# The first stage of a layered state-space and feed-forward kernel: where four small steps stand

## What is computed

```
x = x + 0.5 * (layernorm(x) @ w.T + bias)          # w: 6-bit weights, (q - zero_point) * scale
x = x + causal_convolution(layernorm(x), K0) + D0 * layernorm(x)
x = x + 0.5 * (layernorm(x) @ w.T + bias)
x = x + 0.5 * (silu(n @ W_gate.T) * (n @ W_up.T)) @ W_down.T      # n = layernorm(x)
x = x + causal_convolution(layernorm(x), K1) + D1 * layernorm(x)
x = x + 0.5 * (silu(n @ W_gate.T) * (n @ W_up.T)) @ W_down.T
```

```
denom = g[:, None] - Lambda[None, :]
cauchy = lambda v: (v[None, :] / denom).sum(-1)
k00, k01, k10, k11 = cauchy(Ct.conj() * B), cauchy(Ct.conj() * p), cauchy(q.conj() * B), cauchy(q.conj() * p)
K = ifft(c * (k00 - k01 * (1.0 / (1.0 + k11)) * k10)).real
```

## Time and profile before

| | before |
|---|---|
| runs, us | 920.75, 920.38, 916.86 |
| profiled execution, us | 920.42 |
| its span, first to last instruction, us | 918.6 |
| TensorE matmul busy | 888.6 us, 97% |
| VectorE busy | 619.8 us, 67% |
| ScalarE busy | 313.5 us, 34% |
| GpSimd busy | 365.2 us, 40% |
| mean granted TensorE clock | 0.989 |

### The profile page before, as it was taken

One profiled execution on the slowest core, in us unless ns is written; L12 is line 12 of the kernel. 1 busy time (PEld: TensorE's weight loads), 2 busy tenths in 40 slices (PEclk: granted clock), 3 DMA queues, 4 the chain that ended last, 5 costly groups with the idle time before them and its releaser, 6 DMA issues.

```text
span 918.6 us, 11736 instructions
## 1 busy us (share of the span) xinstructions
PE 888.6 (97%) x4116; PEld 725.4 (79%) x4116; DVE 619.8 (67%) x1057; ACT 313.5 (34%) x517; POOL 365.2 (40%) x729
## 2 busy tenths in 40 slices
PE   7899999989999999999999999999999999999998
PEld 3777887777777787888888888888888778888876
DVE  7768778788888878555566786655656864544452
ACT  4423446633443444221223352222243512222211
POOL 4974467832323336232324453233243542222211
PEclk8989999999999999999999999999999999999999
DMA  8200000055676596556465665556455757566345
GB/s 329 91 1 1 1 1 2 1 226 180 238 272 223 216 330 181 153 180 177 133 185 145 189 181 172 184 136 193 150 164 164 227 157 225 191 206 206 126 147 174
DMA packets 41310, 148.27 MB, mean 161 GB/s; under 512 B 3490, under 2 KB 3746, under 8 KB 39844
## 3 DMA queue, kind: packets, MB, share of 16 engines
q0 software_dynamic: 29040, 100.93, 36.6%
q1 hardware_dynamic: 12212, 46.59, 13.7%
HBM read 117.36 MB, written 30.15 MB: 161 GB/s over the span
## 4 chain that ended last, share of the span: by engine, by line
PE 74%; DVE 13%; POOL 7%; issue 2%; DMA 2%; ACT 1%; SPq 0%; DVEq 0%; POOLq 0%; ACTq 0%
PE front L1436 14%; PE front L1438 13%; PE front L1437 13%; PE acc L1390 7%; PE acc L1392 7%; PE acc L1391 7%; PE front L468 3%; DVE weight_operands L600 2%; PE acc L1321 2%; PE acc L1322 2%; PE acc L1320 2%; DVE snapshots L1191 2%; POOL x_rows L748 2%; DVE hidden_lo L1231 2%; POOL rstd L450 1%
## 5 line engine op out<-in xcount | busy, mean ns | idle before, releaser
L1436 PE MATMUL front<-row_operands_hi,weight_operands 128*128 128x512 f32 x616 | 243.2, 395 | 8.2 <-DVE snapshots L1191 8.1
L1438 PE MATMUL front<-row_operands_hi,weight_operands 128*128 128x512 f32 x616 | 240.5, 390 | 0.0
L1437 PE MATMUL front<-row_operands_lo,weight_operands 128*128 128x512 f32 x616 | 240.4, 390 | 0.0
L1436 PEld LDWEIGHTS front<-row_operands_hi,weight_operands 128*128 128x128 f32 x616 | 116.0, 188 | 36.5 <-issue 10.1
L1390 PE MATMUL acc<-down_weights,hidden_hi 128*128 128x512 f32 x352 | 140.0, 398 | 3.9 <-DMA down_weights<-saved_down 2.0
L1191 DVE TENSOR_TENSOR snapshots<-front,snapshots 128x512 f32<-128x512 f32 x132 | 90.9, 689 | 78.3 <-PE front L1438 77.0
L1392 PE MATMUL acc<-down_weights,hidden_lo 128*128 128x512 f32 x352 | 137.4, 390 | 0.0
L1391 PE MATMUL acc<-down_weights,hidden_hi 128*128 128x512 f32 x352 | 137.2, 390 | 0.0
L1438 PEld LDWEIGHTS front<-row_operands_hi,weight_operands 128*128 128x128 f32 x616 | 116.0, 188 | 24.7
L1437 PEld LDWEIGHTS front<-row_operands_lo,weight_operands 128*128 128x128 f32 x616 | 116.1, 189 | 23.3
L820 POOL DMA_DIRECT2D weight_operands<-saved_weights x66 | 48.6, 736 | 185.5 <-PE front L1438 180.6
(11 more groups left out here) (177 smaller groups left out, 1349.3 us busy)
## 6 DMA issues: line engine op xcount, KB each, us to landing
weight_operands<-saved_weights POOLq DMA_DIRECT2D x33, 1280.0 KB, 6.4
down_weights<-saved_down POOLq DMA_DIRECT2D x77, 512.0 KB, 4.1
saved_weights<-weight_operands SPq DMA_DIRECT2D x11, 1792.0 KB, 8.2
weight_operands<-saved_weights POOLq DMA_DIRECT2D x33, 512.0 KB, 4.5
raw_weights<-wgu SPq DMA_DIRECT2D x11, 512.0 KB, 4.3
saved_down<-down_weights SPq DMA_DIRECT2D x11, 512.0 KB, 3.4
x_rows<-x_in SPq DMA_DIRECT2D x3, 1024.0 KB, 11.6
out<-x_rows SPq DMA_DIRECT2D x3, 1024.0 KB, 5.1
```

The costliest lines, as they stand in the source:

```text
L1436: T.matmul(o, wh, xh, start=(j == 0), stop=False)
L1437: T.matmul(o, wh, xl, start=False, stop=False)
L1438: last = T.matmul(o, wl, xh, start=False, stop=(j == 1))
```

## The change

Four edits, all in the first stage:

- The numerators are split. The 12 small products and sums (`numerators`) now stand after the second `rstd_step` and before `dequant_lo(0)`; the 8 copies and sign changes into the right sides (`right_sides`) stand after `dequant_lo(1)`. The wait for the statistics of item 8 between them is gone.
- The sum of the squares is made by VectorE, directly before the first reciprocal (n = 3), and no longer by GpSimd.
- The first 16 items rotate over three sums banks, acc 0, 1 and 3, and products(n) waits for update n - 3. Items 16 to 18 wait for one update more than before.
- At n = 0 TensorE makes no transposes; behind the products of n = 1 it makes those of items 4 and 5.

```diff
@@ sum_bank
-            return acc[l % 2] if l < TILES else acc[(l + 1) % (BLK - 1)]
+            return acc[(0, 1, 3)[l % 3]] if l < TILES else acc[(l + 1) % (BLK - 1)]
@@ GpSimd
-                pool.wait_ge(rstd_ready, NUMERATORS_AT + RSTD_AHEAD + 1)
+            def right_sides():
                 for layer in range(2):
...
             rstd_step(pool, 0)
             rstd_step(pool, 1)
+            numerators()
             dequant_lo(0)
             rstd_step(pool, 2)
             rstd_step(pool, 3)
             dequant_lo(1)
+            right_sides()
...
-                if n == NUMERATORS_AT:
-                    numerators()
-                if n == 2:
-
-                    pool.wait_ge(den_squared, 2)
-                    TT(mag[:], mag[:], tmp[:], ALU.add).then_inc(mag_ready, 1)
@@ VectorE, reciprocal(c)
+                if c == 0:
+                    dve.wait_ge(den_squared, 2)
+                    V.tensor_tensor(mag[:], mag[:], tmp[:], ALU.add).then_inc(mag_ready, 1)
@@ TensorE
-                    if 2 <= l < TILES:
+                    if TILES <= l < TILES + 3:
                         pe.wait_ge(light_updated, l - 1)
-                    if l >= TILES:
+                    elif l >= 3:
                         pe.wait_ge(light_updated, l - 2)
...
-                if n + XT_AHEAD < PRE:
+
+                if n == 1:
+                    transpose_step(pe, XT_AHEAD)
+                if n and n + XT_AHEAD < PRE:
                     transpose_step(pe, n + XT_AHEAD)
```

More of the change, by code:

```diff
@@ L733, in dequant_lo @@
                 TT(Ql[:, j, :], wq[:, j, :], Qh[:, j, :].bitcast(F32), ALU.subtract).then_inc(dequant_split, 1)
[L735 to L751, removed]
             def numerators():
@@ L776, in numerators, with bias_step @@
                     pool.wait_ge(numer_ready, (layer + 1) * 4)
+            rstd_step(pool, 0)
+            rstd_step(pool, 1)
+            numerators()
+            dequant_lo(0)
+            rstd_step(pool, 2)
+            rstd_step(pool, 3)
+            dequant_lo(1)
+            right_sides()
+            for n in range(XT_SLOTS, RSTD_AHEAD):
+                rstd_step(pool, n)
+            def bias_step(n):
+                pool.wait_ge(norm_done, n + 1)
+                nc.gpsimd.tensor_tensor(x_tile(ITEMS[n].tile), x_tile(ITEMS[n].tile), biasB[:], ALU.add
+                                        ).then_inc(bias_added, 1)
             def invert(c):
```

## The result

| | before | changed |
|---|---|---|
| runs of the first session, median (range), us | 920.16 (916.86 to 921.81), 8 runs | 913.94 (912.86 to 918.46), 8 runs |
| profiled execution, us | 920.42 | 918.46 |
| span, us | 918.6 | 916.7 |
| mean granted TensorE clock | 0.989 | 0.987 |

The ratio is 0.9945, 95% interval 0.9929 to 0.9961. In two later sessions the changed kernel came to 0.9967 (0.9946 to 0.9987) and 0.9963 (0.9947 to 0.9979). So it is faster by 0.3 to 0.6%, some 3 to 5 us. Its executions spread over 5 to 7 us in each session, which widens these intervals; in the first two sessions they lie in two groups, near 913 and near 918 us, in the third they fill the space between as well. The profiled one is the slowest of the first session.

What follows compares the result with a forecast made beforehand. GpSimd's queue before the Cauchy products was taken as the bound: 4.9 - 0.3 - 0.3 = 4.3 us earlier there, 3.6 us after the slower clock, so 920.4 - 3.6 = 916.8 us, range 913.6 to 919.6.

Steps and rivals of the forecast that it cites:

- Where the bound lies: First stage: GpSimd's last inversion, ending at 55.8 us before the change, lets the Cauchy products start and sets the stage.
- TensorE's part: Reordered transposes and a third sums bank bring TensorE to the Cauchy products at 47.8 us, against 54.1; no gain by itself.
- GpSimd's queue: Between 24 and 56 us, 4.9 us of work leaves GpSimd; its last inversion comes 4.3 us earlier, at 51.6 us.
- disturbance: VectorE's new sum of squares slows GpSimd's instructions beside it: 0.3 us, between 0 and 0.7.
- The start term: Numerators and right sides, moved early in GpSimd's queue, delay the kernel's start by 0.3 us, between 0.1 and 0.8.
- VectorE's sum: The sum of squares on VectorE at about 36 us takes 0.68 us and costs nothing on VectorE.
- cover of 4 us: VectorE's fourth reciprocal is done at about 46 us, where GpSimd wants it at about 50.
- The clock at the Cauchy products: After a 3.8 us wait, Cauchy products run at the lower clock for 3.4 us and tile 9's products take 5.1 us.
- a sign of an error in size: Slow clock stretches differing from the 3.4 us and 6.8 us of before would show the predicted size wrong.
- rival (a): Around the Cauchy products and tile 9 the clock falls later or recovers sooner; 915.3 us for a 3 us earlier recovery; chance 0.22.
- bound without any fall: If the clock never falls at the Cauchy products and tile 9, the time is bounded by 913.4 us.
- Rival (c): The gain does not show, as a resource outside TensorE's chain keeps its time or the start costs more; 919.5 to 920.4; chance 0.07.

Runs made afterwards that it cites:

- changed_again: The changed kernel's same code, profiled and timed a second time in a later session; ratio to the kernel before 0.9967, median 917.92 us.
- changed_third: The changed kernel's same code, profiled and timed a third time in another session; ratio to the kernel before 0.9963, median 917.08 us.
- cauchy_one_later: The changed kernel with the Cauchy products and everything that hangs on them one tile later; ratio to the kernel before 0.9941.
- gpsimd_edits_only: The changed kernel without TensorE's two edits, so only the numerators, right sides and sum of squares are moved; ratio to the kernel before 0.9940.
- filled_both: The changed kernel with 13 filling matmuls before the Cauchy products and 8 before the Toeplitz products; 913.31 us, ratio to the kernel before 0.9934.

## Why the prediction held, point by point

- Where the bound lies. That GpSimd's last inversion sets the Cauchy start was right, and shown from both sides: relieved alone it gives the whole gain, and TensorE's edits alone give nothing.
- TensorE's part. Cauchy products reached at 47.8 us foreseen, 47.7 measured; tile 5's transposes to end at 25.4, ended at 25.3. No update was late.
- GpSimd's queue. 4.9 us out less 0.3 for the start less 0.3 for disturbance, 4.3 foreseen. The corrected Cauchy start moved from 55.9 to 51.2, 4.7 us, but it leaves the start out and is to be set beside 4.9 - 0.3 = 4.6. The numerators took 2.27 us as worked out, and the right sides were hidden (3.24 us idle behind them). The start term can be read from VectorE's first use of the weights (L1011 before, L1004 after) to tile 0's update: 8.71 to 26.51 us before, 8.04 to 26.21 in the first profile, 0.37 us longer, all of it in the shift that ran beside the low part; in changed_again and changed_third 0.08 and 0.09 us longer. So the 0.3 us was right for the first profile and too large for the other two. From that same point to the Cauchy products the gain is 4.4, 4.6 and 4.6 us. Beside the new VectorE sum (35.84 to 36.50 us) a GpSimd instruction took 0.24 in place of 0.19 us: 0.05 us and not 0.3. In cauchy_one_later it was 0.45 us at the sum, so this term depends on how the instructions of the two engines fall beside each other. The 1.0 us that GpSimd lost there beside VectorE's denominators, which stood there before the change too, was in no term of the prediction.
- VectorE's sum. 0.68 us foreseen from L1033, 0.66 measured, and its cover of 4 us was there.
- The clock at the Cauchy products. In the first profile this came near to what was worked out: the Cauchy products and tile 9 wholly at 1.2 GHz, tile 9's transposes at 59.56 (60.1 foreseen), the wait for the twist 1.81 (2.0), the Toeplitz start 71.92 (72.1), the lead 3.8 (3.6). Two misses cancel in it. The Cauchy products started 0.7 us earlier than foreseen (50.86, not 51.6). And the slow stretch was 10.2 us long, which the prediction had itself named a sign of an error in size: it reached into tile 9's transposes, which took 0.98 us in place of 0.60, and VectorE waited 0.71 us and not 0.36 for the rounded rows behind them. But this was one of three cases: in the two other profiles rival (a) happened, the clock came back within tile 9, and the lead was 6.2 us net of the start. I gave (a) 0.22; by three profiles it is not less likely than the forecast. Its bound without any fall was also too small. I put 0.7 us on the Cauchy products, from a row in which they were already partly slow; wholly at the high clock they take 1.8 us (52.34 to 54.15 in gpsimd_edits_only), which is 1.6 us less than 3.4, and filled_both, with no fall, had a lead of 7.7 us at 190 us where the bound of 913.4 us allows 7.0.
- From 76 to 190 us the lead is carried unchanged, as foreseen. Rival (c) fell. The step I did not have is what the clock does later: two slow stretches, at 197 and 719 us, fall or do not fall in a given execution, at 1 to 2 us each. From 190 to 375 us the first profile loses 0.5 us, while changed_again and changed_third, without the first stretch, gain 1.1 and 0.6 us on the kernel before, which has it; by 756 us the first profile loses 1.9 us more and the other two 0.2 and 0.4. The first stretch follows a wait of 2.18 to 2.19 us for VectorE, which stands in all four traces, also in the two where the clock held; before the second TensorE waits 1.4 to 1.8 us for a load of down weights.
- The time. 916.8 us foreseen, 913.94 in the first session, 917.92 and 917.08 in the later ones. By ratio 3.6 us is 0.9961, which lies at the edge of the first interval and within the other two. The first session's median is 2.9 us below the forecast and lies near the lower end of the range, which stood there for case (a) and not for the forecast; that the number was hit owes something to that width, and to luck. The 0.5% border of faster is crossed by the first session's ratio, though not by its whole interval, and not by the others, so 0.62 for the same and 0.33 for faster was about what the chip says.
- Rival (d), slower by a clock that stays down, did not occur: the longest slow stretch was 10.2 us.

## What to carry to other kernels

Where several engines meet at one point, work out the arrival of each. Only the last one's queue is worth shortening, and there each instruction counted about one to one at the start of the next stage, however small; in the time of the whole kernel 1.2 us of it could not be seen. Making an early engine earlier is not free on TensorE: its longer wait can bring the clock down for the work behind it, so an edit worth nothing in the sum can cost 2 to 4 us, as in one pair of kernels here. The better moves are to take work off the late engine until the arrivals match, or, if they can't match, to give TensorE something to do. After such a move, do the sum again at the next meeting point before you count the gain.

## What the runs showed of the hardware

The same wait of 3.1 to 3.2 us before the same instructions was followed by 3.4 us at 1.2 GHz in two executions and by 10.2 us in another. With the 16-column Cauchy products behind them, a wait of 1.39 us was followed by 6.8 us and one of 0.50 us by 3.4 us, while a wait of 1.79 us before the Toeplitz products was followed by none. Even the same wait of 2.18 us near 195 us was followed by 3.4 us at 1.2 GHz in the changed kernel's first profile and by none in its third. So the length of a wait does not by itself tell whether the clock falls. One profile is therefore no measure of a change of 0.5%: three profiles of one kernel spread over 5 us, while their Cauchy starts agree within 0.1 us once the start of the stage is taken off. To compare two traces, the start of the same instruction in each, less the difference at the beginning, was the sharper tool.
